# Mixture-of-experts kernel: earlier down weights, three passes from tile 4, halved last reads

## What is computed

```python
h = einsum('bsi,bio->bso', x, W[id]) + b[id]            # one of 16 matrices for each sequence
y = (silu(h @ sw1) * (h @ sw3)) @ sw2                   # shared, inner width 352
weights, indices = top_k(softmax(h @ gate_w), 2)        # 8 experts, 2 for each token
for e in range(8):                                      # routed, inner width F = 176
    y += cw[:, e:e+1] * ((silu(h @ rw1[e]) * (h @ rw3[e])) @ rw2[e])
out = x + y
```

## Time and profile before

| | |
|---|---|
| time, median of 3 runs | 127.83 us (126.64 to 127.92) |
| the profiled execution | 127.45 us |
| its span, first to last instruction | 125.8 us |
| PE busy | 105.3 us (84%) |
| DVE, ACT, POOL busy | 62.2, 45.0, 46.9 us |
| moved by DMA | 19.07 MB, mean 152 GB/s |
| mean granted TensorE clock | 0.949 |

### The profile page before, as it was taken

The page is one execution under the profiler, slowest core; times in us unless marked ns, Lnnn a source line. Parts: engine busy times, 40 slices in busy tenths (PEclk is TensorE's granted clock), DMA queues, the critical chain, the costliest instruction groups (busy, mean ns, idle before and its releaser), DMA issues.

```text
span 125.8 us, 2009 instructions
## 1 busy us (share of the span) xinstructions
PE 105.3 (84%) x554; PEld 85.2 (68%) x554; DVE 62.2 (49%) x202; ACT 45.0 (36%) x111; POOL 46.9 (37%) x63
## 2 busy tenths in 40 slices
PE   6698999999993990079999999999999996999600
PEld 4477887678882560057777778899998994888400
DVE  1045567899822021004675676455555543126992
ACT  4145676612320161005677563454344432001100
POOL 4450378787740000003335433534435344600520
PEclk9999999999999599657999999999999999999995
DMA  3888999952225589951222332331021210029824
GB/s 92 258 272 257 346 348 372 387 205 83 106 106 134 145 188 222 209 180 56 76 91 77 109 118 85 121 114 42 10 83 39 75 50 0 6 46 376 328 87 163
DMA packets 16593, 19.07 MB, mean 152 GB/s; under 512 B 2323, under 2 KB 13447, under 8 KB 16583
## 3 DMA queue, kind: packets, MB, share of 16 engines
q1 hardware_dynamic: 13158, 12.62, 33.5%
q0 software_dynamic: 1984, 4.46, 10.0%
q10 hardware_dynamic: 1440, 1.86, 4.6%
HBM read 12.64 MB, written 7.21 MB: 158 GB/s over the span
## 4 chain that ended last, share of the span: by engine, by line
PE 53%; DMA 17%; POOL 9%; DVE 7%; issue 7%; SPq 2%; ACT 1%; POOLq 1%; DVEq 0%; ACTq 0%
PE bank L774 35%; DMA raw<-in_L_ffn_rw_dram 11%; POOL rows_by_expert L369 7%; DVE x_area L751 6%; PE bank L786 6%; PE bank L943 4%; PE bank L908 3%; DMA y_area<-_out_by_choice_and_token 3%; DMA rows_by_expert<-h_area,slot 2%; DMA _out_by_choice_and_token<-y_area,dest 2%; SPq L310 1%; PE bank L801 1%; PE bank L804 1%; ACT hT_hi L413 1%; POOL cond_area L267 1%
## 5 line engine op out<-in xcount | busy, mean ns | idle before, releaser
L382 POOL DMA_INDIRECT _out_by_choice_and_token<-y_area,dest x23 | 22.7, 986 | 51.1 <-DVE y_area L716 51.1
L774 PE MATMUL bank<-raw,gT_f 88*128 x92 | 24.9, 393 | 7.9 <-DMA raw<-in_L_ffn_rw_dram 6.8
L774 PEld LDWEIGHTS bank<-raw,gT_f 88*128 88x128 f32 x92 | 17.3, 195 | 12.1 <-issue 9.0
L369 POOL DMA_INDIRECT rows_by_expert<-h_area,slot x16 | 16.2, 1012 | 11.2 <-DVE slot L590 7.1
L480 ACT COPY gT_f<-bank 88x256 f32<-88x256 f32 x23 | 8.5, 369 | 25.9 <-PE bank L943 25.9
L716 DVE COPY y_area<-bank 128x256 f32<-128x256 f32 x23 | 9.8, 425 | 14.7 <-PE bank L774 14.7
L774 PE MATMUL bank<-raw,hsT 128*128 x44 | 17.0, 514 | 0.0
L710 DVE TENSOR_TENSOR y_area<-y_area,bank 128x176 f32<-128x176 f32 x23 | 7.8, 338 | 18.3 <-ACT y_area L476 18.3
L774 PE MATMUL bank<-w_all,hsT_hi 128*128 x48 | 14.4, 343 | 0.0
L476 ACT ACTIVATE y_area<-bank 128x176 f32<-128x176 f32 x23 | 7.3, 318 | 12.0 <-PE bank L774 11.4
L908 PE MATMUL bank<-ident,h_area 128*128 128x128 f32 x46 | 9.4, 287 | 2.0 <-DMA h_area<-rows_by_expert 2.0
(11 more groups left out here) (118 smaller groups left out, 151.4 us busy)
## 6 DMA issues: line engine op xcount, KB each, us to landing
h_area<-rows_by_expert SPq DMA_DIRECT2D x23, 128.0 KB, 2.1
raw<-in_L_ffn_rw_dram SPq DMA_DIRECT2D x16, 176.0 KB
raw<-in_L_ffn_rw_dram SPq DMA_DIRECT2D x2, 704.0 KB
rows_by_expert<-x_area SPq DMA_DIRECT2D x8, 128.0 KB
y_area<-_out_by_choice_and_token SPq DMA_DIRECT2D x4, 256.0 KB, 4.6
y_area<-_out_by_choice_and_token ACTq DMA_DIRECT2D x4, 256.0 KB, 5.2
out_dram<-x_area SPq DMA_DIRECT2D x4, 256.0 KB, 2.0
sh_raw<-in_L_ffn_sw_dram SPq DMA_DIRECT2D x2, 352.0 KB, 5.2
```

The costliest lines, as they stand in the source:

```text
L369: nc.gpsimd.indirect_dma_start(out=rows_dram, out_offset=bass.IndirectOffsetOnAxis(ap=slot[:, i, t:t + 1], axis=0), in_=h_sb[:, t, :], in_ ...
L382: nc.gpsimd.indirect_dma_start(out=y_dram, out_offset=bass.IndirectOffsetOnAxis(ap=dest[:, j:j + 1], axis=0), in_=y_sb[j % NBY], in_offset ...
L774: last = nc.tensor.matmul(dst, w, v, start=start and n == 0, stop=stop and n == len(operands) - 1)
```

## The change

- The raw2 and sh2_raw loads are issued by SP right behind the filling's writes, before SP waits for the tile starts; all eight first tile reads follow one another.
- `sh_lo` of the narrow columns is computed by DVE (behind the last `hT_lo`) instead of POOL.
- `FIRST_SPLIT` is 4 instead of 11. The eight hi parts are made by ACT in pairs behind the shared SiLUs of groups 1 to 4, the lo parts by DVE: one before gate 4, two before gate 5, two behind it, and three in steps 0 to 2 of the loop.
- TensorE runs `table()` before `turn_rows(0)`, and at step 23 `turn_gated(22)` before `down(21)`.
- The reads back of the first and the last sequence are halved (one token tile each, 128 KB), each half with its own semaphore; DVE weighs a half completely before the next; the last sequence is stored in halves.

```diff
-    FIRST_SPLIT = 11
+    FIRST_SPLIT = 4
...
-        y_in = [sem(f"y_in{b}") for b in range(B)]
+        pieces = [JS if b in (0, B - 1) else 1 for b in range(B)]
+        y_in = [[sem(f"y_in{b}_{n}") for n in range(pieces[b])] for b in range(B)]
...
+        def read_rows(queue, i):
+            for b in range(B):
+                for n in range(pieces[b]):
+                    cols = slice(n * JS * D // pieces[b], (n + 1) * JS * D // pieces[b])
+                    queue.dma_start(y_tok[:, b, i, cols], y_by_choice[i, b][:, cols]).then_inc(y_in[b][n], 16)
...
@@ SP @@
             for e in range(E):
                 sp.dma_start(rows_dram[e * ROOM:e * ROOM + P, :], x_sb[:, 0, 0, :]).then_inc(filled, 16)
+            for c in range(2):
+                sp.dma_start(raw2[:, :, c, :],
+                             rw2[:, c * FH:(c + 1) * FH, :].rearrange("e p d -> p e d")).then_inc(raw2_in, 16)
+            sp.dma_start(sh2_raw[0:M0, 0, :], sw2[FS - M0:FS, :]).then_inc(sh2_in, 16)
+            sp.dma_start(sh2_raw[:, 1:NSH, :], sw2[0:FS - M0, :].rearrange("(c p) d -> p c d", p=P)).then_inc(sh2_in, 16)
...
-            for j in range(NBH // 2):
+            for j in range(NBH):
                 load_tile(j, first_starts[j])
-            for c in range(2):
-                sp.dma_start(raw2[:, :, c, :],
-                             rw2[:, c * FH:(c + 1) * FH, :].rearrange("e p d -> p e d")).then_inc(raw2_in, 16)
-            for j in range(NBH // 2, NBH):
-                load_tile(j, first_starts[j])
-            sp.dma_start(sh2_raw[0:M0, 0, :], sw2[FS - M0:FS, :]).then_inc(sh2_in, 16)
-            sp.dma_start(sh2_raw[:, 1:NSH, :], sw2[0:FS - M0, :].rearrange("(c p) d -> p c d", p=P)).then_inc(sh2_in, 16)
...
-            for b in range(B):
-                sp.dma_start(y_tok[:, b, 0, :], y_by_choice[0, b]).then_inc(y_in[b], 16)
-            for b in range(B):
+            read_rows(sp, 0)
+            for b in range(B - 1):
                 sp.wait_ge(out_ready, JS * (b + 1))
                 sp.dma_start(out_tiled[b], x_sb[:, b].rearrange("p j d -> p (j d)")).then_inc(out_stored, 16)
+            for j in range(JS):
+                sp.wait_ge(out_ready, JS * (B - 1) + j + 1)
+                sp.dma_start(out_tiled[B - 1][:, j * D:(j + 1) * D], x_sb[:, B - 1, j, :]).then_inc(out_stored, 16)
...
@@ POOL @@
-            dispatch(0)
-            pool.wait_ge(sh_hi_ready, 1)
-            nc.gpsimd.tensor_tensor(sh_lo[:, :, shared_cols(0)], sh_raw[:, :, shared_cols(0)],
-                                    sh_hi[:, :, shared_cols(0)].bitcast(F32), ALU.subtract).then_inc(sh_lo_pool, 1)
-            for b in range(1, B):
+            for b in range(B):
                 dispatch(b)
...
@@ ACT @@
             for g in range(len(groups)):
                 shared_silu(g)
+                if 1 <= g <= E // 2:
+                    w13_hi_of(2 * g - 2)
+                    w13_hi_of(2 * g - 1)
...
-                if 1 <= s <= E:
-                    w13_hi_of(s - 1)
...
-            for b in range(B):
-                act.dma_start(y_tok[:, b, 1, :], y_by_choice[1, b]).then_inc(y_in[b], 16)
+            read_rows(act, 1)
...
@@ DVE @@
             hT_lo_of(3, 1)
+            sh_lo_of(0)
             two_highest_of(2)
...
+            w13_lo_of(0)
             shared_gate(4)
+            w13_lo_of(1)
+            w13_lo_of(2)
             shared_gate(5)
+            w13_lo_of(3)
+            w13_lo_of(4)
             dve.wait_ge(table_ready, 1)
...
-                if 2 <= s < E + 2:
-                    w13_lo_of(s - 2)
+                if s + 5 < E:
+                    w13_lo_of(s + 5)
...
+            def weigh(b, i, j):
+                t = JS * b + j
+                if i == 1:
+                    dve.wait_ge(combining, t + 1)
+                nc.vector.scalar_tensor_tensor(
+                    out=x_sb[:, b, j, :], in0=y_tok[:, b, i, j * D:(j + 1) * D],
+                    scalar=weight[:, t, i:i + 1], in1=x_sb[:, b, j, :],
+                    op0=ALU.mult, op1=ALU.add).then_inc(combining if i == 0 else out_ready, 1)
             for b in range(B):
-                dve.wait_ge(y_in[b], 16 * TOPK)
...
+                for n in range(pieces[b]):
+                    dve.wait_ge(y_in[b][n], 16 * TOPK)
+                    for i in range(TOPK):
+                        for j in range(n * JS // pieces[b], (n + 1) * JS // pieces[b]):
+                            weigh(b, i, j)
...
@@ PE @@
-            turn_rows(0)
             table()
+            turn_rows(0)
             for s in range(NTILE + 2):
...
                 if s < NTILE:
                     up(s)
+                if s == NTILE:
+                    turn_gated(s - 1)
                 if 0 <= s - 2:
                     down(s - 2)
-                if 0 <= s - 1 < NTILE:
+                if 0 <= s - 1 < NTILE - 1:
                     turn_gated(s - 1)
```

More of the change, by code:

```diff
@@ L216, in adaln_moe_ffn @@
         sh_hi_ready = sem("sh_hi_ready")
-        sh_lo_pool = sem("sh_lo_pool")
-        sh_lo_dve = sem("sh_lo_dve")
+        sh_lo_ready = sem("sh_lo_ready")
         htok_ready = sem("htok_ready")
@@ L329, in _ @@
                 sp.wait_ge(scattered[i], 16 * len(range(i, NTILE, NBY)))
-            for b in range(B):
-                sp.dma_start(y_tok[:, b, 0, :], y_by_choice[0, b]).then_inc(y_in[b], 16)
-            for b in range(B):
+            read_rows(sp, 0)
+            for b in range(B - 1):
                 sp.wait_ge(out_ready, JS * (b + 1))
                 sp.dma_start(out_tiled[b], x_sb[:, b].rearrange("p j d -> p (j d)")).then_inc(out_stored, 16)
-            sp.wait_ge(out_stored, 16 * B)
+            for j in range(JS):
+                sp.wait_ge(out_ready, JS * (B - 1) + j + 1)
+                sp.dma_start(out_tiled[B - 1][:, j * D:(j + 1) * D], x_sb[:, B - 1, j, :]).then_inc(out_stored, 16)
+            sp.wait_ge(out_stored, 16 * (B - 1 + JS))
         @block.gpsimd
@@ L460, in _ @@
             nc.scalar.preload_act_table(ACT.Silu)
-            for g in range(len(groups)):
-                shared_silu(g)
-            def hsT_of(j):
-                act.wait_ge(hsT_ps_ready, j + 1)
-                nc.scalar.copy((hsT if j < FIRST_SPLIT else hsT_hi)[j % 2][:, :], hsT_ps[j % 2]).then_inc(hsT_ready, 1)
             def w13_hi_of(e):
@@ L472, in w13_hi_of, with hsT_of @@
                 nc.scalar.copy(w_all[:, e, HI13:LO13], raw13_rows[:, e, :]).then_inc(w13_hi_ready, 1)
+            for g in range(len(groups)):
+                shared_silu(g)
+                if 1 <= g <= E // 2:
+                    w13_hi_of(2 * g - 2)
+                    w13_hi_of(2 * g - 1)
+            def hsT_of(j):
+                act.wait_ge(hsT_ps_ready, j + 1)
+                nc.scalar.copy((hsT if j < FIRST_SPLIT else hsT_hi)[j % 2][:, :], hsT_ps[j % 2]).then_inc(hsT_ready, 1)
             def sil_of(j):
@@ L594, in sh_lo_of @@
                 dve.wait_ge(sh_hi_ready, c + 1)
-                lo_part(sh_lo[:, :, cols], sh_raw[:, :, cols], sh_hi[:, :, cols]).then_inc(sh_lo_dve, 1)
+                lo_part(sh_lo[:, :, cols], sh_raw[:, :, cols], sh_hi[:, :, cols]).then_inc(sh_lo_ready, 1)
             def at_row_of(first, last):
@@ L601, in at_row_of, with w13_lo_of @@
                 ready.then_inc(at_row_ready, 1)
+            def w13_lo_of(e):
+                dve.wait_ge(w13_hi_ready, e + 1)
+                lo_part(w_all[:, e, LO13:ROW], raw13_rows[:, e, :], w_all[:, e, HI13:LO13]).then_inc(w13_lo_ready, 1)
             def base_of(b):
@@ L720, in hsT_lo_of @@
                 lo_part(hsT_lo[j % 2][:, :], hsT_ps[j % 2], hsT_hi[j % 2][:, :]).then_inc(hsT_lo_ready, 1)
-            def w13_lo_of(e):
-                dve.wait_ge(w13_hi_ready, e + 1)
-                lo_part(w_all[:, e, LO13:ROW], raw13_rows[:, e, :], w_all[:, e, HI13:LO13]).then_inc(w13_lo_ready, 1)
             for s in range(NTILE + 2):
@@ L745, in _ @@
                     dve.wait_ge(late_base_ready, b - BH + 1)
-                for i in range(TOPK):
-                    for j in range(JS):
-                        t = JS * b + j
-                        if i == 1:
-                            dve.wait_ge(combining, JS * b + j + 1)
-                        nc.vector.scalar_tensor_tensor(
-                            out=x_sb[:, b, j, :], in0=y_tok[:, b, i, j * D:(j + 1) * D],
-                            scalar=weight[:, t, i:i + 1], in1=x_sb[:, b, j, :],
-                            op0=ALU.mult, op1=ALU.add).then_inc(combining if i == 0 else out_ready, 1)
+                for n in range(pieces[b]):
[3 more added lines that the diff above has]
+                            weigh(b, i, j)
         @block.tensor
@@ L811, in shared_up @@
                 if w == 0:
-                    if c == 0:
-                        pe.wait_ge(sh_lo_pool, 1)
-                    else:
-                        pe.wait_ge(sh_lo_dve, c)
+                    pe.wait_ge(sh_lo_ready, c + 1)
                 if g < 3:
```

(2 more changed lines are left out.)

## The result

The changed kernel takes 118.28 us (median of 4, 117.59 to 119.06) against 127.8 before: a ratio of 0.928, 95% interval 0.919 to 0.936. The profiled execution took 117.91 us with a span of 116.3, so 9.54 us less than the profiled one of before; 117.0 had been predicted, from 112.8 to 121.2. Medians are over all executions of a kernel, ratios and their intervals over those within 1.5% of its fastest.

What follows compares the result with a forecast made beforehand. TensorE was taken to wait 6.85 us for raw2, then set the pace, losing time at half clock. Terms -6.85 - 2.0 - 1.61 - 0.6 - 0.6 + 1.2 = -10.5 took 127.45 to 117.0 us, range 112.8 to 121.2.

Steps and rivals of the forecast that it cites:

- Part 1, the wait: TensorE's idle time until raw2 lands, ahead of the first down products: earlier loads remove it, -6.85 us.
- the second dip: TensorE's half-speed stretch at 51.45 to 58.28, around its wait for raw2: goes with that wait, -2.0 us.
- Part 1, the price: First tile reads queue behind raw2 and sh2_raw; with sh_lo moved, first transposes at 41.5 instead of 40.27, +1.2 us.
- no queueing: Rival at the first tile: raw2 flows beside the row writes, tile 0 lands at 39.65; 113.5 us, chance 0.27.
- adding up: Rival at the first tile: row writes and raw2 add up, tile 0 at 43 to 45; 120.2 to 122.7 us, chance 0.23.
- Flow of raw2: Raw2's load behind the filling keeps its old rate, 1.44 MB in 11.9 us, 121 GB/s.
- The first dip: TensorE's half-speed stretch near the first tile: kept with its 1.7 us; gone if tile by 40.3, second if by 43.
- Part 2, sh_lo to DVE: POOL's row writes before the first tile: 0.9 us sooner, less 0.3 from DVE subtractions beside them, -0.6 us.
- Part 3: Three passes from tile 4: tiles 4 to 10 take 2.26 instead of 2.49 us each, -1.61 us.
- Part 4: Last tile: tile 22's transposes ahead of down 21, so the last scatter starts sooner, -0.6 us.
- Part 5: Tail with halved reads and stores: sooner first reads -0.9, weighings +0.6, shorter last store -0.3; together -0.6 us.
- The dependent pairs: Tail weighings that wait for the one just before, four pairs losing 0.15 us each: +0.6 us.

Runs made afterwards that it cites:

- e10: Kernel before with only the raw2 and sh2_raw loads moved behind the filling, on the third chip; median 120.02 us.
- e3: Changed kernel with raw2 issued behind tile 3's read and sh2_raw behind tile 7's again; median 126.65 us, ratio 0.986.
- e11: Changed kernel plus 20 unread matmuls before the first tile, whole tail reads and stores, w13_lo 0 behind gate 4, sh2_raw behind tile 7; third chip, 115.07 us, ratio 0.909.
- e1: Changed kernel run again without any edit; median 118.10 us, ratio 0.924.
- e2: Changed kernel with whole instead of halved reads and stores in the tail; median 116.92 us, ratio 0.922.
- e4: Changed kernel with DVE's lo part 0 moved behind gate 4 and lo part 2 behind gate 5; median 118.38 us, ratio 0.919.
- e9: Changed kernel run a third time without any edit, on the third chip; median 118.71 us.
- e12: Changed kernel plus 20 unread matmuls before the first tile and whole tail reads and stores only; third chip, median 115.98 us, ratio 0.916.
- e8: e6 with FIRST_SPLIT back at 11, on the second chip; median 123.56 us, ratio 0.992.
- e6: Same edits to the changed kernel as e11, but run on the second chip; median 122.28 us, ratio 0.984.
- e5: Changed kernel plus 20 unread matmuls between table() and turn_rows(0), on the second chip; median 123.10 us, ratio 0.989.

## Why the prediction was right, step by step

**Part 1, the wait: right.** 6.85 us and the second dip were to go. Both are gone from the waits and the strip. Part 1 alone is worth 6.9 us in medians (e10), 8.0 in traces (127.45 against 119.40) and 8.7 between fastest executions; the sum gives -6.85 - 2.0 less the about 1 us by which the first tile comes later (41.27 against 40.27), 7.85.

**Part 1, the price: right in size, wrong in its mechanism.** The prediction let tile 0's read queue behind raw2 and sh2_raw, as in the earlier trace rows. It does not. The first reads, issued at 38.69, landed in normal time (h_area after, reads issued in 36 to 42), as in the earlier trace rows:

```profile
DMA to landing us min/median/max: 1.9/2.1/2.1
```

The late ones are POOL's row writes, for which SP waits before it reads. The windows of after:

```profile
30.00:34.00 4.00, 4.00 (x19) 3.26 (x18) 4.00 (x15) 2.35 (x4) 2.94 (x3) 1.00 0.87 282
...
36.00:38.00 2.00, 2.00 (x10) 1.41 (x8) 1.77 (x3) 0.60 (x1) 0.00 (x0) 1.00 0.63 237
38.00:40.00 2.00, 0.58 (x17) 0.47 (x16) 1.72 (x3) 0.00 (x0) 0.00 (x0) 1.00 0.09 14
```

The engines, 0.28 busy with the writes in the earlier trace rows, are 0.87 busy, and the last write is over (38.47) when the loads are: by 38 to 40 the share is 0.09. The last write landed 2.40 us after its start before, as its chain of waits has it:

```profile
35.46 2.40 DMA rows_by_expert<-h_area,slot
```

With the loads gone (e3) the same write lands in 3.15 us, of which 0.76 is POOL's hold; with them it took 4.2 to 6.2; with sh2_raw alone taken away (and no hold, e11) some 3.7. So the step that failed is "the tile reads now stand behind 1.44 MB": by the time SP may read, the loads are through. What "no queueing" and "adding up" both lacked is that the delay falls on the writes. It also spreads more than thought: transposes at 40.7 to 42.7 over six traces with all four loads early and the new POOL order (after, e1, e2, e4, e9, e12). SP's four issues took 4.9 us instead of some 2 (22.95 to 27.88), without consequence, since SP then waits for the row writes.

**Flow of raw2: too slow in the sum.** It was taken at its old 121 GB/s. Beside the writes 282 GB/s were moved in 30 to 34, and the writes alone made 99 before: about 180 GB/s for both loads together, an estimate from these two windows. Raw2's own rate among them is not shown. In e11, with raw2 alone early, the DMA share is down to 0.41 in 36 to 37, where after's is 0.87.

**The first dip: right in size, not in its border.** It was kept with 1.7 us, with a second stretch if tile 0 came only by 43. From the first transposes to the last scatter, traces without half speed take 56.0 to 56.2 us (e2, e11, e12), the one with 3.41 us of it 57.75 (after), those with 6.8 us 58.4 to 58.8 (e1, e4, e9): 1.7 us for the first stretch, as the earlier trace rows gave it, and 0.7 to 1.1 for the second, part of which lay in idle time in e1 and e4. But the border was not a time of tile 0: before, with the first transposes at 40.27, had the stretch, and e2, at 40.68, had none. Nor was it the idle time alone. Longer idle times mostly had more (2.04 us none in e2, 2.27 one in after, 2.54 two in e4, 3.03 and 4.08 two in e1 and e9), but 2.05 us had one before and 3.08 us one in e10. Why one execution has it and the next has not, stays open. With TensorE kept busy, e11's and e12's traces have none ahead of the tail.

**Part 2, sh_lo to DVE: right in sum, both pieces mis-sized.** POOL gained 1.3 us, not 0.9: the last write starts at 34.14 instead of 35.46. The hold by a two-input DVE subtraction, read off at 0.44 for one write and set at 0.3, was 0.76 for the last one, where it counts most. Where the loads are late the two give 0.6 as predicted: first transposes at 39.69 in e3, 40.27 before. While the loads are in flight neither visibly moves the landing (e4, e10).

**Part 3: right.** The period is 2.26 from tile 4 on and no wait for a lo part appears; e8 against e6 gives 1.61 in traces and 1.3 in medians, for 1.61.

**Part 4: right.** Down 22 follows down 21 and the last scatter starts straight behind the one before it, with 0.30 between (after, POOL's timeline):

```profile
97.31 0.98 POOL L385 DMA_INDIRECT _out_by_choice_and_token<-y_area,dest  x1 [0.91 <-DVE y_area L729]
98.60 0.99 POOL L385 DMA_INDIRECT _out_by_choice_and_token<-y_area,dest  x1 [0.30 <-issue]
```

The idle time ahead of it was 0.91 in the earlier trace rows: -0.61, for -0.6 predicted.

**Part 5: wrong, +1.1 for -0.6.** The sooner start was right (-0.8 for -0.9). The two terms against it were the wrong ones. The dependent pairs, set at +0.6, cost next to nothing: in after twelve weighings take 5.98 us, 0.50 each, the length of one from the pairless run of the earlier trace rows. What was not in the sum is that all later sequences land later when the first is read in halves. "DVE's 16 weighings fill DVE to the end" was true of the kernel before and was taken over; from the fourth weighing on it no longer held, and DVE stood 2.39 us. The weighings took 10.6 us in all (103.56 to 114.17) instead of 8.4, and the last store, half as long, landed in 1.7 us instead of 2.0: -0.8 + 2.2 - 0.3 = +1.1. Halved tails take 17.7, 17.7, 17.7, 17.1 and 17.3 us (after, e1, e3, e4, e9), and 16.6 in e5; whole ones take 16.6, 16.7, 16.5, 16.6 and 16.6 (before, e2, e10, e11, e12).

In sum: -10.5 predicted, -9.5 measured; the tail is 1.7 worse and the first tile 0.6 better than set. That the total lies so near is in part luck. Two errors partly cancel, and the price of +1.2 stands for a delay that came about in another way. Single executions of the changed kernel took 115.72 to 120.45 us, over half of the forecast's range, so the time alone would not have told the forecast from its rivals; the traces do. How much of that the clock made can be estimated: e9's fastest and slowest execution had a mean granted clock of 0.975 and 0.951, so 5.7 and 11.6 us at half speed, which accounts for at most 3.0 of the 4.7 us between them.

The Trainium skill, DMA: Bandwidth & Descriptors, section Why a DMA increments its semaphore by 16 and not by 1, gave the prediction its rule for the number of engines, by which raw2's 88 partitions are spread over 11. The estimate from it had raw2 through before any tile is read, and 115.2 us. No tile read queued, but raw2 was not through by 32: in e11, where it is the only such load, 237 GB/s still flow in 35 to 36, and 106 flowed there before. The row writes paid for it. How many engines served raw2 was not tested.

## What to carry to other kernels

Moving a load off the critical queue is worth the wait it ends, but look at everything that moves on the DMA engines in the stretch it goes to, and at who waits for that; here it was the indirect writes, not the reads behind the load. Halving a read helps its first consumer and can starve the next: add up when each later piece lands before you count the gain. Where TensorE must idle two or three microseconds ahead of its long loop, a few unread matmuls in the gap are cheap: they made half-speed stretches rare, and the best kernel (115.07 us) has them. Count them against the gap: where there was none (e5) they cost about their own 2.2 us.

## What the hardware showed that was not expected

- The landing of an indirect write of 128 rows depends on what else flows: 2.40 us before, 3.13 to 6.21 with the last of 1.8 MB of loads beside it.
- One DVE subtraction of 0.87 us with both inputs in SBUF stretches POOL's indirect write from 0.96 to 1.72 us, so by nearly its whole length.
- Reads with runs of 1 KB in DRAM among those of 2 KB: the DMA engines stay over 80% busy and the bytes fall from 367 and 406 to 191 and 164 GB/s.
- Idle times of 2.0 to 2.5 us ahead of the first tile led to none, one or two half-speed stretches of 3.4 us. With TensorE kept busy in that gap ten of twelve executions had a mean granted clock of 0.974 or more, without it two of 28.
- On one chip of three DVE stood idle for 1.3 to 7.3 us in routing or in the shared network without a releaser in the profile, in the traces of four kernels; the cause stays open.
